# Graph network on one core: the last scatter of each row of edge counts with 114 entries instead of 128

## The reference

```python
h = relu(layernorm(x)); x = x + L0(h)   # m = h[src] + edge_attr_96; aggr = segment_sum(m, dst); MLP
h = relu(layernorm(x)); x = x + L1(h)   # relu(h[src] + edge_attr_32 @ We + be), segment_sum, MLP, batch norm
h = relu(layernorm(x)); x = x + L2(h)   # 3 GCN layers: out = segment_sum(norm * hw[src], dst) + b
h = relu(layernorm(x)); x = x + L3(h)   # 3 attention layers, 4 heads: softmax over the edges of a node
```

## Time and profile before

| | us |
|---|---|
| median of 3 runs | 12,588.94 |
| the 3 runs | 12,553.91, 12,599.67, 12,588.94 |
| span of the profiled execution | 12,571.5 |

### The profile page before, as it was taken

One profiled execution on the slowest core, in us unless ns is written; L12 is line 12 of the kernel. 1 busy time (PEld: TensorE's weight loads), 2 busy tenths in 40 slices (PEclk: granted clock), 3 DMA queues, 4 the chain that ended last, 5 costly groups with the idle time before them and its releaser, 6 DMA issues.

```text
span 12571.5 us, 140237 instructions
## 1 busy us (share of the span) xinstructions
PE 6178.3 (49%) x36085; PEld 5371.9 (43%) x36085; DVE 5097.4 (41%) x15838; ACT 4054.9 (32%) x10426; POOL 7982.0 (63%) x8396
## 2 busy tenths in 40 slices
PE   0199731255555567999344444433444334443443
PEld 0188621234444445777333333333334333343333
DVE  8455400033222224222444444444444444444444
ACT  0199400034444440000333333333333323333332
POOL 1877777557777750000677777667777766777775
PEclk8555665666666667999555555555555555555555
DMA  8044421222222214666222222222222222222222
GB/s 278 17 103 104 126 83 39 56 44 53 53 53 53 53 38 131 210 209 217 63 68 68 67 68 68 56 66 68 67 68 68 67 54 67 68 68 68 67 68 59
DMA packets 1053014, 1038.73 MB, mean 83 GB/s; under 512 B 641834, under 2 KB 758358, under 8 KB 1052336
## 3 DMA queue, kind: packets, MB, share of 16 engines
q1 hardware_dynamic: 704544, 611.05, 16.6%
q0 software_dynamic: 264160, 337.47, 13.2%
q10 hardware_dynamic: 83664, 82.78, 2.0%
HBM read 935.74 MB, written 96.55 MB: 82 GB/s over the span
## 4 chain that ended last, share of the span: by engine, by line
POOL 60%; issue 21%; PE 11%; DVE 4%; ACTq 2%; DMA 1%; ACT 0%; DVEq 0%; POOLq 0%; SPq 0%; PEldq 0%
POOL sb_HG L565 47%; POOL edge_counts L626 13%; PE sums L975 3%; ACTq L651 2%; PE psA L975 1%; PE psB L975 1%; PE sums L912 1%; PE psD L975 1%; PE psC L975 1%; PE psA L860 1%; DVE sb_ACC L1942 0%; PE psD L894 0%; PE psD L870 0%; PE psC L870 0%; PE psB L886 0%
## 5 line engine op out<-in xcount | busy, mean ns | idle before, releaser
L565 POOL DMA_INDIRECT sb_HG<-attention_table,sb_NOW x4992 | 4731.8, 948 | 1574.4 <-issue 1516.5
L912 PE MATMUL sums<-sb_HG 128*128 128x100 f32 x9984 | 2068.6, 399 | 443.9 <-ACT sb_HG L695 426.6
L912 PEld LDWEIGHTS sums<-sb_HG 128*128 128x128 f32 x9984 | 2035.4, 313 | 453.9 <-ACT sb_HG L695 435.6
L626 POOL DMA_INDIRECT edge_counts<-sb_HG x1625 | 1632.3, 1005 | 764.8 <-issue 495.0
L691 ACT ACTIVATE sb_H<-sb_iota_row,sb_H 128x128 f32<-128x128 f32 x6656 | 2029.1, 388 | 137.7 <-PE sums L912 63.9
L565 POOL DMA_INDIRECT sb_HG<-feature_table,sb_NOW x1612 | 1522.0, 944 | 556.3 <-issue 490.8
L1942 DVE TENSOR_TENSOR sb_ACC<-sb_ACC,sums 128x100 f32 x4992 | 1274.1, 255 | 1152.5 <-PE sums L912 619.0
L922 PEld LDWEIGHTS sums<-sb_HG 128*128 128x128 f32 x6656 | 1324.8, 299 | 315.4 <-issue 315.4
L922 PE MATMUL sums<-sb_HG 128*128 x6656 | 1340.6, 384 | 144.0 <-ACT sb_HG L695 71.3
L760 ACT ACTIVATE psC<-sb_SB 128x128 f32<-128x128 f32 x156 | 43.8, 281 | 3935.1 <-DVE sb_SB L1895 3935.1
L1487 DVE TENSOR_TENSOR sb_ACC<-sb_ACC,sums 128x97 f32 (+1 forms) x3328 | 848.0, 255 | 605.1 <-PE sums L922 135.9
(11 more groups left out here) (442 smaller groups left out, 9019.0 us busy)
## 6 DMA issues: line engine op xcount, KB each, us to landing
sb_HG<-edge_counts SPq DMA_DIRECT2D x1152, 256.0 KB, 3.3
sb_H<-rel_rows SPq DMA_DIRECT2D x312, 512.0 KB
sb_HG<-attention_table,sb_NOW POOLq DMA_INDIRECT x4992
sb_HG<-in_edge_attr_dram SPq DMA_DIRECT2D x201, 384.0 KB, 3.5
edge_counts<-sb_LW ACTq DMA_DIRECT2D x12, 6272.0 KB, 42.5
edge_counts<-sb_HG POOLq DMA_INDIRECT x1625
sb_HG<-feature_table,sb_NOW POOLq DMA_INDIRECT x1612, 2.5
sb_EA<-in_edge_attr_dram SPq DMA_DIRECT2D x201, 128.0 KB, 2.5
```

The lines of the kernel that those rows point to most:

```text
L565: pool.indirect_dma_start(to, None, rows, bass.IndirectOffsetOnAxis(ap=index, axis=0)).then_inc(landed, 16)
L626: pool.indirect_dma_start(every_count, bass.IndirectOffsetOnAxis(ap=slot_of[:, f:f + 1], axis=0), tally[:, f:f + 1], None).then_inc(scatte ...
L912: last = nc.tensor.matmul(bank[:, k // 4, k % 4 * width:(k % 4 + 1) * width], HOT[:, hot, k, :], G[:, slot, k, 0:width], start=True, stop= ...
```

## The change

For each row p, the loop over its 13 columns now goes by chunk number, and the last chunk takes the partitions 0 to 113 in place of 0 to 127: `EF - 128 * 12` is 114. The other 12 scatters of a row are as before, and so are their order, the waits and the increments of the semaphores. The sort, the tables and the spare group are not changed.

```diff
@@ -622,9 +622,10 @@
                 if n == EARLY:
                     load_windows()
                 for p in range(ROWS_TOGETHER * n, ROWS_TOGETHER * (n + 1)):
-                    for f in range(p, SORTED, P):
-                        pool.indirect_dma_start(every_count, bass.IndirectOffsetOnAxis(ap=slot_of[:, f:f + 1], axis=0),
-                                                tally[:, f:f + 1], None).then_inc(scattered[n % 2], 16)
+                    for c in range(CHUNKS):
+                        f, rows = P * c + p, min(P, EF - P * c)
+                        pool.indirect_dma_start(every_count, bass.IndirectOffsetOnAxis(ap=slot_of[0:rows, f:f + 1], axis=0),
+                                                tally[0:rows, f:f + 1], None).then_inc(scattered[n % 2], 16)
                 if n:
                     landing(n - 1)
             landing(LANDINGS - 1)
```

## The result

| | median us | runs | lowest to highest |
|---|---|---|---|
| before | 12,596.56 | 18 | 12,553.91 to 12,604.67 |
| after | 12,616.55 | 18 | 12,589.73 to 12,627.28 |

The ratio after to before is 1.0016, 95% interval 1.0009 to 1.0023: 20 us more (11 to 29). That is under the 0.5% that I had set as the bound for a measurement, but 18 runs of each tell it from nothing, and it goes the other way than forecast.

A forecast was written before the change was run, and what follows sets the result against it. GpSimd's issue of 1,625 scatters was taken as the bound. Terms: -6 us for the instruction, 0 for gaps, DMA engines and long scatters, against the 12,588.94 median, giving 12,583 us; whole range 12,550 to 12,690.

The forecast's parts named there:

- What bounds the kernel: Stage of 1,625 scatters: only GpSimd holds it, at 1,264 ns each; a microsecond there moves the stage's end by a microsecond.
- The DMA engines hide everything: Scatter stage: leaving out 1,750 writes gains nothing on the DMA engines, busy 1.9%; the 2.13 us last landing would need thirtyfold growth.
- the costing of the short scatter: The 125 scatters cut to 114 entries: about 50 ns saved on each, 6 us in all, gaps of 0.30 us unchanged.
- Both bounds that I took for the forecast: Short scatters: at most 105 ns saved each (13 us) if time is proportional to entries, 0 if fixed per instruction.
- The rival of the uneven deal: Short scatters: 6 engines with 19 entries each, 19 steps instead of 8, costing 41 to 165 us; chance 0.26.
- The saving of 0 that I worked out from it: Short scatters: by the skill's "small, variable" descriptor generation, the saving is at the lower bound, 0, and the time 12,589.
- My sign for the uneven deal: Scatter group: every 13th longer, mean up by up to 101 ns, last start 41 to 165 us later, 1,250 packets fewer.
- the three prices that I had listed: Steps making up all, half or a quarter of the 959 ns scatter: 165, 82 or 41 us more.
- the forecast's own range: Whole kernel: 12,550 to 12,600 us around the forecast of 12,583, with the scatter of the runs.
- Within 0.5%: Whole kernel: time the same to within 63 us, chance 0.78, summed as 0.43 + 0.28 + 0.07.
- a saving: Short scatters: some part of the price goes by entry, so 1 to 13 us less; chance 0.43.
- a fixed price: Short scatters: the instruction costs 959 ns whatever the entries, so 0 us change and 12,589 us; chance 0.28.

## Why the prediction was wrong

**What bounds the kernel: right.** The stage is GpSimd's, its issue is the path, and each change moved the end by what it did to GpSimd: 19.3 us for a measured 20, and in the experiments 257 for 258, 315 for 315, -180 for -186.

**The DMA engines hide everything: right for this change.** The last landing took 2.45 us against 2.13. Only in the kernels with far more steps in a batch did GpSimd pause (below).

**The step that failed** is in the costing of the short scatter, "Between the two I take about half, 50 ns a scatter: 125 x 0.05 = 6 us". Both bounds that I took for the forecast, 0 and 105 ns saved, supposed that fewer entries can't cost more; the case in which they do stood only among the rivals. The price follows the entries of the busiest engine, and that number rises from 8 to 19 when 128 becomes 114. Measured: +151 ns on the scatter in place of -50, and +28 ns on the one behind it, for which the sum had no term at all.

**The rival of the uneven deal was the right mechanism.** 6 engines with 19 entries each, in steps, as it said. Its size was off: a step costs 16 ns between 16 and 128 entries, 13.3 between 114 and 127, and 17 between 119 and 114, not 60 or 120. The steps are about an eighth of the 959 ns, where the rival decided only from 38% on, so even the right mechanism stays below 63 us: at a quarter it gave 41 us, and it came out at half of that. The rows could not have decided it: with no count but 128 in the trace, they bound what a scatter can save, and say nothing of the sign.

**The rule of the Trainium skill** that I set beside it ("DMA: Bandwidth & Descriptors", section "Why a DMA increments its semaphore by 16 and not by 1": the largest number of engines up to 16 that divides the slowest dimension) holds in every count tried, as the packet sizes read: 6 for 114, 7 for 119, 13 for 117, 15 for 120, 1 for 127, and 16 for 16, 112 and 128. The exception for direct copies that it names did not apply to these indirect ones. The same section says that all 16 engines add to the semaphore whatever the shape, and in all kernels GpSimd's queue has 16 packets of 4 bytes for each indirect DMA. The other sentence that I cited, from the section "Anatomy of one DMA — SWDGE (gpsimd) path" of that page of the Trainium skill, that the generation of descriptors is "small, variable" and that many can be emitted before the added cost shows, fits equal shares: 113 ns between 16 and 128 entries. It does not fit the others: 151 ns more for 14 entries fewer, and 1.58 us more for one fewer. The saving of 0 that I worked out from it did not come.

**My sign for the uneven deal was wrong in one point.** I said that the packets would fall by 1,250. They did not fall at all, since idle engines get fillers. Every 13th scatter is longer and the mean has risen by 11 ns, as it said. The last start is later, but by 19.3 us and not by the 41 to 165 of the three prices that I had listed.

**The range and the chances.** 12,616.55 lies in the range of 12,550 to 12,690, but outside the forecast's own range of 12,550 to 12,600. It is 33.6 us above the 12,583 forecast: 6 for the saving that did not come, 20 for the cost that did, and 7.6 because the kernel before itself has a median of 12,596.56 over 18 runs where I had three. "Within 0.5%" had 0.78 and came, and that was luck: 0.71 of it stood on a saving and on a fixed price, neither of which held, and only 0.07 on the uneven deal at a small price.

**What stays open.** The price by the step is right in the large, not to 10 ns: one step cost 9 ns between 120 and 119 entries throughout (83 ns for 9 steps), 12 between 117 and 119, and 27 between 128 and 112. Why 120 entries cost 30 to 38 ns more than 128 at the same steps, and 117 less than 120 at one step more, is not settled; that the fillers cost something is only argued. Nor is the reason for the 14 to 28 ns behind a scatter with another count: it is paid after the return to 128, twice as much where the count before did not fill 16 engines, and no run shows what GpSimd does in it.

## What to carry to other kernels

For an indirect DMA from GpSimd keep the number of entries a multiple of 16 (16, 112 and 128 were tried), and pad to it where the padding has a harmless place to go: 14 useless entries are 151 ns cheaper than leaving them out, and 127 in place of 128 costs 1.6 us. Entries dealt in equal shares to all 16 engines are nearly free (113 ns for 112 of them, 1 ns each), instructions are not (some 830 ns and a gap of 300). That fewer instructions would pay follows from these prices; no run here tried it. When a cost has never been seen at the new size, ask what the size is divided into before taking it as proportional.

## What the runs showed of the hardware

Two things I had not expected. First, the fillers: engines that get no entry still get descriptors, 10 packets of 76 bytes for each scatter of 114, so that the changed kernel, with fewer entries, moved 0.09 MB more.

Second, the pauses. In three kernels GpSimd stopped for 2 to 5 us once in each batch of 65 scatters, 25 times, and never in the others. With one descriptor for each step and one for the semaphore, the sum over the batch up to the pause was 51 x 20 = 1,020 (all 114), 4 x 128 + 56 x 9 = 1,016 (127 at the row's end) and 56 x 18 = 1,008 (all 119, foretold); one scatter more passes 1,024 in each. The scatters of the kernels without a pause stay at 640 or less in a batch. Counted in this way, the bound lies between 1,020 and 1,024, which speaks for a queue of about 1,024 descriptors for each engine whose count starts anew with each batch. Why it starts anew there was not tested. It is not that GpSimd waits for a landing: between the first batch and the second it waits for nothing (the first landing is waited for behind the second batch), and in front of the third stand the 26 gathers of index windows, behind the last such wait, which at 9 descriptors each would bring the pause 12 or 13 scatters forward if they counted. Yet in all three kernels the pause stands in front of the same scatter in these batches as in the others. What does change at each of these places is the semaphore that the DMAs increment; whether that is the reason is open.
